# Last stage of a ConvLSTM and grouped-convolution kernel: sixteen 32x32 tiles of TensorE in place of shifted copies and 128x32 tiles

## The reference

```python
x = x + L0(gn(x))      # masked 1x3 convolution, then a recurrence over the 32 rows
x = x + L1(gn(x))      # 3x3 convolution
# gn: mean and variance over the 4 channels of a group and all pixels, 32 groups
# L1: W has a 3x3 kernel where (i - n) % 4 == 0 (n output, i input channel),
#     elsewhere only the centre tap; zero padding 1
is3x3 = (i - n) % 4 == 0
Wm = W * where(is3x3, full, center)
y = conv(x, Wm, padding 1) + sum(b, axis=1)
```

## Time and profile before

| | us |
|---|---|
| median of three runs | 649.83 |
| lowest, highest | 649.73, 656.97 |
| the profiled execution | 652.95 |
| its span, first to last instruction | 651.1 |

### The profile page before, as it was taken

The page is one execution under the profiler, slowest core; times in us unless marked ns, Lnnn a source line. Parts: engine busy times, 40 slices in busy tenths (PEclk is TensorE's granted clock), DMA queues, the critical chain, the costliest instruction groups (busy, mean ns, idle before and its releaser), DMA issues.

```text
span 651.1 us, 14360 instructions
## 1 busy us (share of the span) xinstructions
PE 599.2 (92%) x4968; PEld 379.9 (58%) x4968; DVE 510.0 (78%) x1204; ACT 470.3 (72%) x838; POOL 391.8 (60%) x385
## 2 busy tenths in 40 slices
PE   1899899899999999999999999954999999999996
PEld 0344344578888888888888888842333333333332
DVE  5789875389999999999999999997577667677442
ACT  2579878699999999999999999965333433443320
POOL 2379848345555555555555555568667667777761
PEclk9799979899999999999999999995999999999999
DMA  9989920004432344442244443007798998989987
GB/s 232 271 236 268 217 35 0 10 4 65 66 54 35 45 66 65 66 66 41 31 61 65 66 65 57 11 1 190 206 276 253 269 282 248 288 265 270 261 273 204
DMA packets 96423, 89.29 MB, mean 137 GB/s; under 512 B 78240, under 2 KB 79520, under 8 KB 96288
## 3 DMA queue, kind: packets, MB, share of 16 engines
q1 hardware_dynamic: 89152, 69.47, 46.7%
q10 hardware_dynamic: 7200, 18.90, 10.0%
HBM read 35.07 MB, written 16.78 MB: 80 GB/s over the span
## 4 chain that ended last, share of the span: by engine, by line
PE 67%; SPq 13%; DVE 8%; DMA 6%; ACT 3%; issue 2%; POOL 1%; ACTq 1%; DVEq 0%; POOLq 0%
PE ps L1165 18%; PE ps L1143 12%; PE ps L1219 9%; PE ps L1170 9%; SPq L416 8%; PE ps L1147 6%; SPq L422 5%; DMA shifted<-pad 5%; PE ps L1088 5%; PE ps L1089 5%; PE ps L1209 2%; DVE bn L477 2%; DMA ident<-in_consts_dram 1%; ACT xn L899 1%; DVE img L744 1%
## 5 line engine op out<-in xcount | busy, mean ns | idle before, releaser
L823 POOL TENSOR_TENSOR fc<-gate,cell 128x352 f32<-128x352 f32 (+16 forms) x96 | 83.9, 874 | 144.6 <-ACT gate L973 144.6
L854 POOL COPY shifted<-pad 32x1073 f32<-32x1073 f32 x128 | 137.5, 1074 | 54.7 <-DVE pad L737 48.3
L1165 PE MATMUL ps<-z_hi,wg_hi 128*128 128x352 f32 (+13 forms) x384 | 134.2, 351 | 3.1 <-ACT z_hi L957 3.1
L1165 PE MATMUL ps<-z_hi,wg_lo 128*128 128x352 f32 (+13 forms) x384 | 122.4, 320 | 0.0
L1219 PE MATMUL ps<-shifted,wt_hi 128*32 128x512 f16 x1536 | 108.8, 390 | 9.0 <-DMA shifted<-pad 9.0
L1170 PE MATMUL ps<-z_lo,wg_hi 128*128 128x352 f32 (+13 forms) x384 | 107.5, 321 | 0.0
L973 ACT ACTIVATE gate<-ps,gate_bias 128x352 f32<-128x352 f32 (+16 forms) x192 | 104.2, 543 | 1.7 <-PE ps L1170 1.7
L744 DVE SCALAR_TENSOR_TENSOR img<-ps,y_unscale,img 128x512 f32<-128x512 f32 x64 | 47.8, 747 | 71.2 <-PE ps L1219 71.2
L973 ACT ACTIVATE ps<-ps,gate_bias 128x352 f32<-128x352 f32 (+16 forms) x192 | 99.5, 518 | 0.2 <-PE ps L1170 0.2
L1008 ACT ACTIVATE pad<-img,nbias,rstd 128x1024 f16<-128x1024 f32 x32 | 39.9, 1245 | 80.5 <-PE ps L1219 76.1
L833 POOL TENSOR_TENSOR img<-hT,xr 128x352 f32<-128x352 f32 (+1 forms) x96 | 88.8, 925 | 1.7 <-DVE hT L699 1.7
(11 more groups left out here) (121 smaller groups left out, 1116.5 us busy)
## 6 DMA issues: line engine op xcount, KB each, us to landing
shifted<-pad SPq DMA_DIRECT2D x128, 134.1 KB, 4.0
shifted<-pad ACTq DMA_DIRECT2D x128, 134.1 KB, 4.1
xr<-in_x_dram SPq DMA_DIRECT2D x64, 256.0 KB, 5.5
img<-in_x_dram SPq DMA_DIRECT2D x126, 128.0 KB, 3.6
out_dram<-img SPq DMA_DIRECT2D x60, 256.0 KB, 4.3
shifted<-shifted SPq DMA_DIRECT2D x2, 553.5 KB, 6.0
raw_c<-in_L_conv_W_dram SPq DMA_DIRECT2D x4, 144.0 KB, 2.7
out_dram<-img SPq DMA_DIRECT2D x8, 64.0 KB, 1.9
```

The costliest lines, as they stand in the source:

```text
L823: pool.tensor_tensor(fc[it % 2][:, 0:c1 - c0], gate[it % 2][0][:, 0:c1 - c0], cell[:, c0:c1], ALU.mult).then_inc(fc_done, 1)
L854: pool.tensor_copy(shifted[b % SLOTS][32:64, q, ROWS_AT:ROWS_END].bitcast(F32), pad[b % SLOTS][32 * q:32 * q + 32, ROWS_AT:ROWS_END].bitca ...
L1165: pe.matmul(gbank(it, m)[:, 0:n], w[:, GATE_ORDER[m], :], z_hi[it % 2][:, 0:n], start=(w is wg_hi), stop=False)
```

## The change

The padded image is now read directly. A group is a pair of images, cut into four pieces c of 512 pixels (16 rows). Column tile c of the array makes piece c, on PSUM partitions 32c to 32c + 31, and bank q of the group holds output class q. The centre tap runs as 128x32 matmuls, four column tiles together. The eight other taps run on 32x32 tiles (row group q, column group c): input class q from partitions 32q up, piece c, weights `wall[32q.., d, e, 32q..]`. The residual is an f32 matmul with a scaled identity that adds the image into the banks. The evacuation scales and adds the bias, classes 0 and 2 on ACT, 1 and 3 on DVE, and writes the result over the pair in `img32`, from where four DMAs store it. `shifted`, its DMAs and POOL's copies, `place_blocks`, the ones and the bias row are gone; bias and scale per class are made by a small matmul in the first stage. `xn` is in SBUF (two buffers), `pad` has four slots, seven PSUM banks rotate, and eight images' upper statistics are taken in the recurrence. The core of the diff:

```diff
-SLOTS = 3
-POOL_COPIES = 4
-SHIFTS_SP = [(0, 0), (0, 1), (0, 2), (0, 3)]
-SHIFTS_ACT = [(2, 2), (2, 3), (2, 0), (2, 1)]
-XN_BANK = 4
...
+SLOTS = 4
+PAIR = 2
+GROUPS = B // PAIR
+PIECE = PAIR * HW // Q
+PIECE_ROWS = PIECE // W
+Y_BANKS = 7
+TERMS = (("hi", 0), ("lo", 0), ("hi", 1))
+TAPS = [(d, e) for d in range(3) for e in range(3) if (d, e) != (1, 1)]
+ACT_CLASSES, DVE_CLASSES = (0, 2), (1, 3)
...
+        def window(b, part, row, d, e):
+            at = LOW_AT * part + ROWS_AT + (row + d - 1) * PADW + e - 1
+            return pad[b % SLOTS][:, at:at + PIECE_ROWS * PADW].rearrange("p (h w) -> p h w", w=PADW)[:, :, 0:W]
+        def piece(g, c):
+            return PAIR * g + c * PAIR // Q, c * PIECE_ROWS % H
+        def y_bank(g, q):
+            return ps[:, (Q * g + q) % Y_BANKS, :]
+        def group_out(g, q):
+            return img32[:, PAIR * g:PAIR * g + PAIR].rearrange("p b h w -> p (b h w)")[:, PIECE * q:PIECE * (q + 1)]
...
+        def store_group(engine, g, pieces):
+            for c in pieces:
+                r = slice(32 * c, 32 * c + 32)
+                b, row = piece(g, c)
+                engine.dma_start(out_q[:, :, b, W * row:W * row + PIECE].rearrange("q n x -> n q x"),
+                                 img32[r, PAIR * g:PAIR * g + PAIR].rearrange("p b h w -> p (b h w)")
+                                 .rearrange("p (q x) -> p q x", q=Q)).then_inc(stored, 16)
...
-            for b in range(B):
-                shift(b)
-                if b % 2 and b > 2:
-                    store_pair(b - 3)
-            store_last(sp, QUARTERS[:2])
-            sp.wait_ge(stored, 16 * Q * (B // 2 - 1 + 4))
+            for g in range(GROUPS):
+                sp.wait_ge(out_act, len(ACT_CLASSES) * (g + 1))
+                sp.wait_ge(out_dve, len(DVE_CLASSES) * (g + 1))
+                store_group(sp, g, range(Q))
+            sp.wait_ge(stored, 16 * Q * GROUPS)
...
-                if ITEMS - CH <= it < ITEMS:
-                    if it == ITEMS - CH:
+                if ITEMS - HELD <= it < ITEMS:
+                    if it == ITEMS - HELD:
...
+                    upper_stats(it - (ITEMS - HELD))
...
-            def residual(b):
-                for s in range(2):
-                    half = image(b)[:, HW // 2 * s:HW // 2 * (s + 1)]
-                    v.wait_ge(conv_done, 2 * b + s + 1)
-                    v.scalar_tensor_tensor(out=half, in0=y_bank(b, s), scalar=y_unscale[:], in1=half,
-                                           op0=ALU.mult, op1=ALU.add).then_inc(sum_done, 1)
+            def finish_class(g, q):
+                v.wait_ge(conv_done, g + 1)
+                v.tensor_scalar(group_out(g, q), y_bank(g, q), finish[:, 1, q:q + 1], finish[:, 0, q:q + 1], ALU.mult,
+                                ALU.add).then_inc(out_dve, 1)
...
+            for b in range(CH, HELD):
+                lower_stats(b)
+            bn_aggr(FIRST_CHUNKS + 1)
+            lo(0)
+            lo(1)
+            chain_mean(FIRST_CHUNKS + 1)
+            lo(2)
+            chain_var(FIRST_CHUNKS + 1)
+            chain_rstd(FIRST_CHUNKS + 1, 1)
+            image_stats_again(HELD)
+            lo(3)
+            image_stats_again(HELD + 1)
+            for g in range(GROUPS):
+                k = (g + 3) // 2
+                chain = g % 2 == 1 and k < CHUNKS
+                near, far = PAIR * (g + 2), PAIR * (g + 5)
+                finish_class(g, DVE_CLASSES[0])
+                if chain:
+                    chain_mean(FIRST_CHUNKS + k)
+                finish_class(g, DVE_CLASSES[1])
+                if far < B:
+                    image_stats_again(far)
+                if chain:
+                    chain_var(FIRST_CHUNKS + k)
+                if near < B:
+                    lo(near)
+                if chain:
+                    chain_rstd(FIRST_CHUNKS + k, k % 2)
+                if far < B:
+                    image_stats_again(far + 1)
+                    if g % 2 == 0:
+                        bn_aggr(FIRST_CHUNKS + (g + 4) // 2)
+                if near < B:
+                    lo(near + 1)
...
+            pool.memset(pad[0][:].bitcast(F32), 0.0).then_inc(pads_zero, 1)
...
+            pool.memset(pad[1][:].bitcast(F32), 0.0).then_inc(pads_zero, 1)
...
             def high(b):
                 if b >= SLOTS:
 
-                    act.wait_ge(pads_used, b - SLOTS + 1)
+                    act.wait_ge(conv_done, (b - SLOTS) // PAIR + 1)
                 else:
...
+                if b >= PAIR:
+                    act.wait_ge(lo_done, b - PAIR + 1)
+                whiten(rows(xn[b % PAIR][:]), b, b // CH % 2, b % CH).then_inc(xn_done, 1)
+            def finish_class(g, q):
+                act.wait_ge(conv_done, g + 1)
+                act.activation(group_out(g, q), y_bank(g, q), ACT.Identity, bias=finish[:, 0, q:q + 1],
+                               scale=finish[:, 1, q:q + 1]).then_inc(out_act, 1)
...
+            act.wait_ge(gn_step, GN_STEPS * (FIRST_CHUNKS + 1))
+            act.wait_ge(row_done, ROW_AHEAD + ITEMS)
+            high(0)
+            high(1)
+            norm(0)
+            norm(1)
+            high(2)
+            norm(2)
+            square_root(FIRST_CHUNKS + 1)
+            high(3)
+            norm(3)
+            act.wait_ge(finish_done, 1)
+            for g in range(GROUPS):
+                k = (g + 3) // 2
+                near = PAIR * (g + 2)
+                for q in ACT_CLASSES:
+                    finish_class(g, q)
+                if near < B:
+                    if near % CH == 0:
+                        act.wait_ge(gn_step, GN_STEPS * (FIRST_CHUNKS + near // CH + 1))
+                    high(near)
+                    norm(near)
+                if g % 2 == 1 and k < CHUNKS:
+                    square_root(FIRST_CHUNKS + k)
+                if near < B:
+                    high(near + 1)
+                    norm(near + 1)
...
+            WALL = {"hi": wall_hi, "lo": wall_lo}
+            def bank_free(g, q):
+                h = Q * g + q - Y_BANKS
+                if h >= 0:
+                    before, cls = h // Q, h % Q
+                    if cls in ACT_CLASSES:
+                        pe.wait_ge(out_act, len(ACT_CLASSES) * before + ACT_CLASSES.index(cls) + 1)
+                    else:
+                        pe.wait_ge(out_dve, len(DVE_CLASSES) * before + DVE_CLASSES.index(cls) + 1)
+            def out_rows(g, q, c):
+                return y_bank(g, q)[32 * c:32 * c + 32, 0:PIECE]
+            def dense(g, terms, first):
+                for q in range(Q):
+                    if first:
+                        bank_free(g, q)
+                    for m, (w, part) in enumerate(terms):
+                        for c in range(Q):
+                            b, row = piece(g, c)
+                            pe.matmul(rows(out_rows(g, q, c)), WALL[w][:, 1, 1, 32 * q:32 * q + 32],
+                                      window(b, part, row, 1, 1), start=first and m == 0, stop=False,
+                                      tile_position=(0, 32 * c), skip_group_check=True)
+            def residual(g):
+                for c in range(Q):
+                    for q in range(Q):
+                        b, row = piece(g, c)
+                        r = slice(32 * q, 32 * q + 32)
+                        pe.matmul(out_rows(g, q, c), ident_y[r, r],
+                                  img32[r, b, row:row + PIECE_ROWS].rearrange("p h w -> p (h w)"), start=False, stop=False,
+                                  tile_position=(32 * q, 32 * c), skip_group_check=True)
+            def tiled(g, terms, last):
+                for m, (w, part) in enumerate(terms):
+                    for d, e in TAPS:
+                        for c in range(Q):
+                            for q in range(Q):
+                                b, row = piece(g, c)
+                                r = slice(32 * q, 32 * q + 32)
+                                ins = pe.matmul(rows(out_rows(g, q, c)), WALL[w][r, d, e, r], window(b, part, row, d, e)[r],
+                                                start=False, stop=last and m == len(terms) - 1 and (d, e) == TAPS[-1],
+                                                tile_position=(32 * q, 32 * c), skip_group_check=True)
+                if last:
+                    ins.then_inc(conv_done, 1)
...
-            dense_half(0, 0)
-            dense_half(0, 1)
-            for b in range(B):
-                if b == 0:
...
+            pe.wait_ge(hi_done, PAIR)
+            dense(0, TERMS[:2], True)
+            sum_means(FIRST_CHUNKS + 1)
+            residual(0)
+            tiled(0, TERMS[:2], False)
+            pe.wait_ge(lo_done, PAIR)
+            sum_vars(FIRST_CHUNKS + 1)
+            dense(0, TERMS[2:], False)
+            tiled(0, TERMS[2:], True)
+            for g in range(1, GROUPS):
+                k = g // 2 + 1
+                chain = g % 2 == 0 and k < CHUNKS
+                if chain:
```

(49 more changed lines are left out.)

229 lines of the change are left out of this document (46 added, 183 removed).

## The result

The changed kernel takes 695.12 us, median of four runs (692.85 to 695.94), where the kernel before takes 650.78 beside it (four runs, 649.73 to 656.97): a ratio of 1.0655, with a 95% interval of 1.0581 to 1.0728. It is slower by 6.6%; forecast was 606 us. The profiled execution took 695.91 us, its span is 694.0.

The account below looks back on a forecast made before the run. TensorE was taken to bound the last stage, DMAs close behind. Group 1 from 460.1, fifteen groups 15 x 9.08 + 6 x 0.6 = 139.8, to 599.9; with the end, span 607.1, 44.0 less; off the median 606 us, range 594 to 645.

Parts of the forecast that it names:

- A pass of sixteen: Last stage: sixteen 32x32 f16 matmuls stream together in 0.222 us; upper bound 0.89 us if only four ever do.
- Dense: Last stage, per group: twelve dense quads at 0.222 us each, 2.66 us.
- the residual: Last stage, per group: one pass of 16 f32 matmuls, 0.85 us.
- Rivals 1, 2 and 4: Column-group loads take turns, 668 us, 0.12; starts at today's rate, 862, 0.08; DVE or ACT bound, 613 to 622, 0.07.
- the rule: Tiled passes: loads overlap only matmuls of another row group, so a pass costs 0.318 us; 643 us, chance 0.05.
- The 62 ns a matmul: Tiled passes: with software decoding, 0.99 us a pass of 16, the time about 900 us.
- The start: Start of the last stage: TensorE starts at 446.0, extra statistics cost 1.0 us, group 1 starts at 460.1.
- The end: After group 15 at 599.9: last evacuations 0.2 + 1.5 us, then 5.5 us for stores; span 607.1.
- the one for the tiled part: Last stage, per group: 24 tiled passes at 0.222 us, 5.33 us, with issue no limit in a burst.
- rival 3: Last stage: instruction packets fetched only when the one before is used; 3 us each, 635 us, worst 700; chance 0.10.
- the pace by the transfer alone: Argument against rival 3: instruction packets follow at their transfer time, 1.0 us each; the tiled part wants one each 1.7 us.
- The last line of the prediction: Tiled passes: the forecast is wrong if sixteen tiles don't stream as one pass.

Follow-up runs that it names:

- the two runs without stores: Changed kernel without the stores of groups 0 to 14, 683.41 us; the same with each term's dense quads ahead of its tiled passes, 677.15 us.
- the run without either: Changed kernel without the stores of groups 0 to 14 and with each term's dense quads put ahead of its own tiled passes: 677.15 us.
- two terms: Changed kernel without the tiled matmuls of the low weights, one of three terms of the outer taps, 672 instructions a group for 928: 644.10 us.
- six loads: Kernel before the change with six superfluous weight loads ahead of each tiled matmul but the first of a half: 778.90 us, beside 655.42.
- spread: Changed kernel with five outer taps in f32 and three in f16, f16 passes and residual spread between the dense terms: 665.95 us, ratio 1.0190.
- blocks: Changed kernel with five outer taps in f32 and three in f16, ordered as dense, f16 taps, residual, f32 taps: 687.21 us, ratio 1.0559.
- half width: Changed kernel with every tiled 32x32 matmul cut to 256 of its 512 columns, same number of instructions: 707.02 us.
- the f16 orders: Changed kernel as it is, 695.12 us, and with each term's dense quads put ahead of its own tiled passes, 690.35 us.

## Why the prediction was wrong

Its steps in turn. **A pass of sixteen** at 0.222 us: right, so the dense and tiled terms stand as array times. Dense is 2.79 us (565.54 to the sum at 568.33), the residual 0.88 for 0.85, each sum 0.31 for 0.3. Rivals 1, 2 and 4 didn't happen, nor did the rule: passes follow by 0.22 us though loads of a tile's own row group stand in between. By the sentence of the Trainium skill ("TensorE: Matmul & The Clock Gate", Part 3) that a weight load overlaps matmuls in flight only when its row group is another, each pass would be longer by a load; the trace of this kernel doesn't agree. The 62 ns a matmul in Part 1 of the same page of the Trainium skill hold where the sequencer decodes in software; at 0.222 / 16 = 14 ns a start, that case isn't this one.

**The start** was near: dense at 446.83 for 446.0, group 1 at 461.61 for 460.1, though GroupNorm's first sum ended 1.9 us later where I took 1.0. **The end**: last matmul to end of span 8.4 us, where the sum had 7.2. These two are 2.7 us.

**The step that failed** is the one for the tiled part, in these words: "in a burst issue is no limit: in 30 ns eight weight loads run and at least four matmuls start". That is true of a burst, and a burst is 256 instructions. A group was sized at 9.3 us and takes 14.93: 15 x 5.6 = 84 us. The mechanism stood there as rival 3, with a chance of 0.10 and 3 us a packet, 635 us, at the worst 700. Its price was the mis-sized term: from 446.83 to 685.6 the stage's 14,850 instructions, 58 packets, took 238.8 us, 4.1 us each. What held the chance down, "the pace by the transfer alone", was no evidence: the earlier trace rows show that a packet takes 1.0 us to move, not how soon the next one may be asked for, and in the kernel before they came 9 us apart (11 in 100 us), so no stretch of it could show a limit. The upper bound should have come from the nearest row of a fetch's whole way, the 4.3 us landing that the prediction itself named, with a share of the chance to match. The last line of the prediction also tested the wrong thing: sixteen tiles do stream as one pass, and the forecast is wrong all the same.

**The 14.9 us, put together:** 928 / 256 = 3.6 packets at 3.7 are 13.4; the stores' delay 0.8; the slow content in one place 0.4 (6.2 / 15 between the two runs without stores). That leaves 0.3; the run without either has 3.78 us a packet behind 465 us, not 3.7, which is this rest. The two small terms come from single runs. What is shown is that the number of instructions and their spacing set the time (two terms; six loads; spread against blocks) and the array doesn't (half width). That one packet is in flight at a time is shown by its start, at each gap at least 1.04 us after the burst on the one before, and by the bursts that broke off, behind which it came later by the wait. Its 3.7 us are 1.1 to its start, 1.1 of transfer and 1.4 to 1.5 to its use. What fills the first 1.1 and the last 1.4 us, and by what stores and copies lengthen the first, is open.

## What to carry to other kernels

Count instructions, not only columns: a stretch of TensorE that uses up 256 instructions (128 matmuls with their loads) in less than about 3.7 to 4.2 us runs out of them here, and the profile shows it as gaps "<- issue" after bursts of 128 matmuls, with the instruction queue's packets evenly spaced. Small tiles pay for packing in instructions: sixteen tiles in one pass are 32 instructions for 0.22 us, four are 8. If such a stretch can't be avoided, mix it finely with slow matmuls (21 us between the two mixed orders, 5 between the f16 orders), and keep large stores away from it.

## What the hardware showed that I had not expected

- Instructions come by DMA while the kernel runs, at most 24 to 27 packets in 100 us here, 61 to 69 instructions a microsecond. The Trainium skill ("Trainium Architecture — The Big Picture", The software stack) has the instruction streams moved to the engines when a program is loaded; the queue view shows them coming through the whole span, 79 packets.
- Stores that keep the DMA engines a third busy delay these packets by 0.8 to 1.4 us a group.
- Superfluous weight loads are not free, but as instructions and not as loads: 210 more a half turned 655 into 779 us, while three passes still took 0.72 us for 0.68.
- An f32 tap on 32x32 tiles takes 1.10 us where the f32 residual, with as many matmuls, takes 0.88. The tap's weights change and its input is a window of a padded image; which of the two makes it isn't shown.
- The granted clock falls below the full 2.4 GHz where TensorE has such gaps: 0.77 at half width (480 to 640 us, busy 70%) and 0.91 with the change in 600 to 680 us (busy 75%), but 0.97 in 500 to 600 us (busy 74%), and 1.00 in the spread order (busy 99%). The busy share alone doesn't tell it.
